# The causal mask of the sixteen single-block score banks moves from a TensorE matmul into the VectorE row-maximum pass

## The reference

```python
H, D = (NUM_HEADS, HEAD_DIM)                      # 16 heads of 8 features
att = jnp.einsum('bqhd,bkhd->bhqk', q, k) * SCALE
mask = _band_mask(T)                              # j > i; the band term adds nothing to it
att = jnp.where(mask[None, None, :, :], -jnp.inf, att)
att = jax.nn.softmax(att, axis=-1)
out = jnp.einsum('bhqk,bkhd->bqhd', att, v).reshape(B, T, C)
```

## Time and profile before

| | |
|---|---|
| median of 3 runs | 1809.23 us (1808.62 to 1812.13) |
| profiled execution, its own time | 1809.41 us |
| span of its trace | 1807.4 us |
| TensorE busy | 1509.6 us (84%), 10072 matmuls |
| VectorE busy | 1187.1 us (66%) |
| ScalarE busy | 859.7 us (48%) |
| GpSimd busy | 546.6 us (30%) |

### The profile page before, as it was taken

One profiled execution on the slowest core, in us unless ns is written; L12 is line 12 of the kernel. 1 busy time (PEld: TensorE's weight loads), 2 busy tenths in 40 slices (PEclk: granted clock), 3 DMA queues, 4 the chain that ended last, 5 costly groups with the idle time before them and its releaser, 6 DMA issues.

```text
span 1807.4 us, 33637 instructions
## 1 busy us (share of the span) xinstructions
PE 1509.6 (84%) x10072; PEld 920.9 (51%) x10072; DVE 1187.1 (66%) x3463; ACT 859.7 (48%) x1787; POOL 546.6 (30%) x626
## 2 busy tenths in 40 slices
PE   2879999999999999999999999999988711447674
PEld 1445656565655556565656565655644311435563
DVE  5477778686878787777868687878756278801110
ACT  0426464646465555646464646555552522423331
POOL 1323222232313132323222231313130120058886
PEclk8879999999999999999999999999997855678888
DMA  2030221213030303031121303030302000044443
GB/s 73 1 82 25 65 55 42 63 32 86 9 88 7 87 16 85 27 68 51 44 57 38 83 13 88 7 87 16 79 26 65 17 2 1 7 93 81 98 84 60
DMA packets 83238, 90.70 MB, mean 50 GB/s; under 512 B 19520, under 2 KB 73024, under 8 KB 78528
## 3 DMA queue, kind: packets, MB, share of 16 engines
q1 hardware_dynamic: 71872, 80.76, 18.0%
q0 software_dynamic: 11264, 8.92, 3.6%
HBM read 58.95 MB, written 29.92 MB: 49 GB/s over the span
## 4 chain that ended last, share of the span: by engine, by line
PE 54%; DVE 17%; issue 12%; POOL 7%; DMA 3%; ACT 3%; SPq 1%; DVEq 1%; POOLq 0%; ACTq 0%
PE fa L702 7%; PE ba L608 6%; PE ba L603 6%; PE fa L694 6%; PE bo L861 6%; PE ba L614 5%; PE fa L712 4%; POOL out L573 3%; PE facc L712 2%; DVE passed L1496 2%; POOL got L543 2%; DVE nm L1286 2%; DMA QT<-nmT 2%; PE ba L981 1%; PE bo L770 1%
## 5 line engine op out<-in xcount | busy, mean ns | idle before, releaser
L1041 ACT ACTIVATE probs<-ba 128x512 f32<-128x512 f32 x640 | 349.6, 599 | 131.7 <-PE ba L614 129.5
L458 POOL TENSOR_TENSOR x<-x,gd 128x512 f32<-128x512 f32 x144 | 182.6, 1268 | 589.8 <-ACT gd L1019 573.3
L603 PE MATMUL ba<-QT,KT 75*128 75x512 bf16 (+3 forms) x1024 | 233.4, 306 | 26.1 <-ACT probs L1041 13.4
L608 PE MATMUL ba<-KT,QT 72*128 72x512 bf16 (+3 forms) x1024 | 230.4, 305 | 7.6 <-DVE nm L1289 3.2
L1286 DVE TENSOR_REDUCE nm<-ba 128x1 f32<-128x512 f32 x256 | 174.4, 681 | 34.2 <-PE ba L614 34.0
L861 PE MATMUL bo<-probs,vp 128*32 128x512 f32 (+3 forms) x2048 | 181.8, 444 | 2.0 <-ACT probs L1041 0.9
L603 PEld LDWEIGHTS ba<-QT,KT 75*128 75x128 bf16 x1024 | 87.5, 100 | 174.4 <-ACT probs L1041 103.4
L702 PE MATMUL fa<-f_nT,w 128*128 128x512 f32 x320 | 170.3, 614 | 3.4 <-DVE hh L1278 3.1
L694 PE MATMUL fa<-f_nT,w 128*128 128x512 f32 x320 | 169.6, 612 | 0.0
L614 PE MATMUL ba<-mask_q,identb 128*128 128x256 bf16 (+1 forms) x640 | 163.8, 256 | 0.0
L614 PE MATMUL ba<-mask_k,identb 128*128 128x256 bf16 (+1 forms) x640 | 163.5, 255 | 0.0
(11 more groups left out here) (279 smaller groups left out, 2668.1 us busy)
## 6 DMA issues: line engine op xcount, KB each, us to landing
QT<-qk_parts SPq DMA_DIRECT2D x96, 192.0 KB
KT<-qk_parts SPq DMA_DIRECT2D x96, 192.0 KB
qk_parts<-qkp SPq DMA_DIRECT2D x32, 384.0 KB, 2.6
fc<-in_L_ffn_fc_weight SPq DMA_DIRECT2D x32, 256.0 KB
xin<-in_L_attn_x SPq DMA_DIRECT2D x16, 256.0 KB, 7.4
qk_parts<-qkp SPq DMA_DIRECT2D x16, 256.0 KB, 2.7
out<-x SPq DMA_DIRECT2D x16, 256.0 KB, 2.3
xn_rows<-row SPq DMA_DIRECT2D x16, 256.0 KB, 7.2
```

The lines of the kernel that those rows point to most:

```text
L458: pool.tensor_tensor(x1[:], x1[:], gd[:, e % 2], ALU.add).then_inc(S["s_x1g"], 1)
L603: pe.matmul(bank[:, col:col + w], lhsT=KT[0:K_ROWS, head, blk * P:(blk + 1) * P], rhs=QT[0:K_ROWS, head, blk * P:], start=first_, stop=False)
L608: pe.matmul(bank[:, col:col + w], lhsT=QT[0:QK_ROWS, head, blk * P:(blk + 1) * P], rhs=KT[0:QK_ROWS, head, 0:w], start=first_, stop=False)
L1041: act.activation(probs[:, pair % 3, f_], ba[n % 3][:], ACT.Exp, scale=SCALE).then_inc(S["s_exp"], 1)
```

## The change

The mask tile for the query-major scores becomes 512 columns wide: zero in its first 384 columns, and in the last 128 the triangle that it held before. For the 16 fills of a batch that hold one row block, the mask matmul is left out, and the score matmul itself ends the group and raises s_S. VectorE takes the maximum of such a bank with tensor_tensor_reduce. It adds the mask tile to the bank, multiplies by -1, writes the 512 results back into the bank, and accumulates their minimum, which is the negative maximum that tensor_reduce gave. The other 24 query-major fills keep their mask matmul and take their mask from the last 128 columns of the wide tile. The key-major fills are as they were. The wide tile lies in the memory region that later tensors reuse.

```diff
-        mask_q = sb("mask_q", [P, P], BF16)
+        mask_q = sb1("mask_q", [P, SEQ], BF16)
...
             const(pool.memset(mask_q[:], 0.0))
-            const(pool.affine_select(mask_q[:], mask_q[:], [[-1, P]], ALU.is_ge, MASKED, base=0, channel_multiplier=1))
+            last_ = mask_q[:, SEQ - P:]
+            const(pool.affine_select(last_, last_, [[-1, P]], ALU.is_ge, MASKED, base=0, channel_multiplier=1))
...
                     w = (blk + 1) * P
-                    pe.matmul(bank[:, col:col + w], lhsT=QT[0:QK_ROWS, head, blk * P:(blk + 1) * P],
-                              rhs=KT[0:QK_ROWS, head, 0:w], start=first_, stop=False)
+                    last = pe.matmul(bank[:, col:col + w], lhsT=QT[0:QK_ROWS, head, blk * P:(blk + 1) * P],
+                                     rhs=KT[0:QK_ROWS, head, 0:w], start=first_, stop=len(groups) == 1)
                     diagonal.append((col + w) // P - 1)
...
-            mask = mask_k if by_key else mask_q
-            last = pe.matmul(blocks, lhsT=identb[:], rhs=mask[:, None, :].to_broadcast([P, n_, P]), start=False, stop=True)
+            mask = mask_k if by_key else mask_q[:, SEQ - P:]
+            if by_key or n_ > 1:
+                last = pe.matmul(blocks, lhsT=identb[:], rhs=mask[:, None, :].to_broadcast([P, n_, P]), start=False, stop=True)
             last.then_inc(S["s_st" if by_key else "s_S"], 1)
...
                 if f in (0, 2):
-                    last = dve.tensor_reduce(nm[:, 3, h:h + 1], bank[:], X, ALU.max, negate=True)
+                    apart(dve)
+                    last = dve.tensor_tensor_reduce(bank[:], bank[:], mask_q[:], -1.0, -MASKED, ALU.add, ALU.min, nm[:, 3, h:h + 1])
```

## The result

The changed kernel takes 1796.74 us (median, 1796.12 to 1798.38) against 1808.92 us for the kernel before on the same chips (1808.16 to 1812.13). The ratio is 0.9928, 95% interval 0.9913 to 0.9944: 12.2 us or 0.7% faster. The forecast was 1799 us.

A forecast was written before the change was run, and what follows sets the result against it. TensorE was taken to bound the middle of each X phase, VectorE its start and tail. 15 x (-0.70) + 0.32 = -10.2 us from 1809.41 gave 1799.2, forecast as 1799 us, range 1796 to 1817.

The forecast's parts named there:

- the sum for one phase: Whole X phase: 3c - 0.03 - 0.79 + 4c - 0.04 + c = 8c - 0.86, or -0.70 us.
- step 2: Middle stretch of the X phase, paced by TensorE: ten removed mask matmuls save 0.79 us per phase.
- the worth of a mask: Each removed mask matmul in the middle stretch saves 0.058 us, or 0.111 in front of `up` or `up3`.
- steps 1 and 3: X phase: +3c - 0.03 us at the start, up to hh(1); later 4c - 0.04 us at `up3(5)`.
- c = 0.02: What one new pass adds to VectorE's pace over the old reduction, in us; taken near a traced row of similar shape.
- 8c per phase: X phase: eight of the sixteen new passes count on the path, 0.16 us at c = 0.02.
- the first two rivals: Accumulator read takes a slot, c = 0.08, 1807 us (16%); write into the bank slows the pass, above 1813 (19%).
- The nop, costed at nothing: No-operation behind the wait on VectorE: no cost, or some 0.05 us without cover.
- Step 3: Middle of the X phase: `up3(5)` waits for VectorE's product hh(4), held for 4c - 0.04, or 0.04 us.
- The last X phase: Last of 16 phases, without expert work, bound by VectorE: masks worth nothing, new passes cost 16c = +0.32 us.

The follow-up runs named there:

- e1_nop_only: The kernel before with only the no-operation added behind the wait of the 16 single-block row maxima per phase, masks kept on TensorE: 1815.14 us, ratio 1.0030.
- e10_after_idle64: The changed kernel with 64 no-operations added on VectorE in idle time of the first stage: 1803.31 us, ratio 0.9962.
- e4_scratch: The changed kernel with the new pass writing its sums to an SBUF tile, not back into the PSUM bank: 1797.01 us, ratio 0.9917.
- e2: The changed kernel with the plain row maximum in place of the new pass, so those maxima leave the mask out: 1802.38 us, ratio 0.9949.
- e6: The kernel before with 32 no-operations added near the start of VectorE's stream: 1826.92 us, ratio 1.0096.
- e7: The changed kernel with 64 no-operations added near the start of VectorE's stream: 1807.62 us, ratio 0.9986.

## Why the prediction was right in part

The direction and the mechanism of the masks held. The step that failed is the sum for one phase: it put the change of VectorE's stream outside the maxima at nothing, without a reason, and there a wait of 0.35 us per pass went away, 4.2 us in all. So the gain was larger than forecast (12.2 us, not 10.2). That the total came so near is luck in part, for the parts that were forecast came out smaller, some 8 us.

**The masks (step 2 and the worth of a mask).** Forecast with steps 1 and 3: 0.86 us per phase. Measured: 0.76, nops included. The price of a pair was right (0.86 us in place of 0.91), and so was the choice of masks that count, since ten do all the work.

**The new pass (c = 0.02, 8c per phase).** Its step of 0.61 us gives c = 0.01, below my figure, so neither the accumulator read nor the write into the bank is the price that the first two rivals had. Yet the sixteen passes cost 0.20 us per phase where I had 0.16. It is 0.0125 for each, so all sixteen count and not eight: counted from the gates, the changed kernel stands 0.04 us behind the run without masks at hh(1), 0.11 at hh(4) and 0.20 at the last maximum. The Trainium skill ("VectorE: DVE Perf Modes", "Two Vector instructions with no wait between them") counts an operation with an accumulator output as two instructions, from which the prediction had estimated c = 0.08. For one pass among reductions the rows do not bear that estimate out. Where passes follow one another they come to 0.05 us each.

**The nop, costed at nothing.** Among the small terms this is the one that failed. Run e1_nop_only has 0.04 us per phase for sixteen, and its rows show where it comes from: behind a wait that is met late, what follows starts 0.07 us later.

**Step 3 (`up3(5)` held by hh(4)).** It was not. `up3(5)` starts at 632.52 on the chain above, and hh(4) ends at 631.49 + 0.68 = 632.17, 0.35 us earlier. The hold fell one step before, at `up3(4)`, whose pair takes 0.95 us on the chain (628.61), 0.09 more than `up3(5)`. Its weight load waits there for VectorE's product hh(3).

```profile
628.43 0.30 PEld L704 LDWEIGHTS fa<-f_nT,w 128*128 128x128 f32 x2 [0.22 <-DVE hh L1280]
```

**The sum for one phase.** Forecast -0.70 us, measured -0.57 without the wait of VectorE. By the measured parts, -0.76 + 0.20 = -0.56.

**The term that was missing.** The sum took all of VectorE's stream outside the maxima as unchanged. The change adds 32 instructions to it per X phase, two for each bank: the nop and the accumulator read. They moved a stall of 0.35 us off the gate scaling ahead of the X phase, in each of the 12 passes of VectorE's loop. (The description ahead of the prediction speaks of thirteen. That is the loop of the other engines; VectorE's runs from 2 to 13.) This is 12 x 0.35 = 4.2 us. The runs that shift the stream alone show it in both directions. Together 15 x 0.57 + 4.2 = 12.8 us, less 0.3 for the last X phase, is 12.5. The medians differ by 12.2, which agrees no better than the last stage allows (below). Without that stall's move the ratio would have been near the 0.9962 of run e10_after_idle64, a gain of some 7 to 8 us and not the 10.2 forecast.

**The last X phase.** Forecast +0.3 us. The stretch over its fills was 25.24 us in before, at a mean granted clock of 0.77 of full speed, and is 27.26 in the profiled execution of the changed kernel. Busy time and granted clock of that stretch, changed kernel first, then run e4_scratch, which differs only in where the pass writes:

```profile
1355.37:1382.63 27.26, 24.46 (x107) 11.26 (x104) 25.49 (x72) 1.19 (x2) 0.92 (x4) 0.65 0.16 36
```

```profile
1355.23:1380.67 25.44, 21.89 (x107) 9.21 (x104) 25.27 (x72) 1.19 (x2) 0.91 (x4) 0.77 0.18 40
```

At a mean clock of 0.77 it is 25.44 us, 0.2 over before, where the forecast had 0.3. At 0.65 it is 27.26, and VectorE waits 1.6 us for TensorE's fills, which it does not in run e4_scratch. Both mix the two levels of the clock, 1.2 and 2.4 GHz. In the X phases before the clock fell TensorE had been busy 39.46 of 40.01 us. What decides in which slices it falls stays open. From the start of this phase to the end it is 437.9 to 441.7 us in the fourteen kernels, mostly the longer the lower its mean clock (0.74 to 0.72). So I compare periods above, and the totals of the mask runs can't be read to the microsecond.

## What to carry to other kernels

Before a gain below 1% is credited to an edit of a program with a hardware loop, run the old kernel with as many idle instructions added on the same engine, and compare the periods of the loop. Replace work on one engine only where that engine is the bound, since ten of these sixteen banks gave all the gain. And price a short operation by its step to the next one in the company in which it will run, not alone.

## What the hardware showed beyond that

**VectorE stalls at fixed places of its own stream.** In this program they lie 128 instructions apart (709, 837, 965 and 1093) and cost 0.35 us at the gate scaling. At the L2 norm, 12 instructions behind the start of a pass, they cost some 0.46 us in e1 and e2 and 1.07 in e6. The page's instruction queue moves 0.66 MB in 80 packets in before (8.2 KB each), and 92 or 93 packets in the runs e1, e2, e6, e7 and e10, the padded or changed ones that have a stall on the path in every pass; the others have 81 to 84. That is about one more fetch for each of the 12 passes. The Trainium skill ("Runtime: NRT & Kernel Launch", "Instruction fetch mechanics") says that instructions come in blocks of 256, that crossing into the next is mostly hidden, and that a taken branch out of the window makes a fetch that is waited for. These traces agree that instructions are fetched in blocks while the loop runs. They differ in the distance, 128. If the places are such crossings, they are not hidden here: the one at the gate scaling costs 0.23% of the time in before. That the fetch itself is what VectorE waits for was argued, not shown. Before has a stall with only 80 packets, and none of them lies at the moment of the stall (614.03 to 614.39 us). What was shown, by instructions that do nothing, is that the place in the stream decides.

**A masked pass may write back into the PSUM bank that it reads** at the pace of a read-only reduction: 0.61 us for 512 columns in place of 0.60.
